# Fourier attention and a mixture of experts: x loaded in quarters, and the early transforms and Nyquist products put in another order

## The reference, cut to what matters

```python
q = layernorm(x) * (scale per token) * (wave per position)
Q, K, V = q @ Wq.T + bq, mem @ Wk.T + bk, mem @ Wv.T + bv
Qf, Kf, Vf = fft(Q), fft(K), fft(V)            # over the 64 positions
QK  = hamilton(Qf * filt, Kf * filt)
QKV = hamilton(QK, Vf * filt)
x = x + ifft(QKV).real
```

## Time and profile before

| | before |
|---|---|
| median of 3 runs | 258.69 us (258.26 to 259.77) |
| the profiled execution | 258.56 us, its trace's span 256.7 us |
| mean granted TensorE clock | 0.895 of full speed |
| busy PE, PEld | 194.5 us (76%), 176.2 us (69%) |
| busy DVE, POOL, ACT | 150.7 us (59%), 142.4 us (55%), 94.5 us (37%) |

### The profile page before, as it was taken

How to read it: one execution, slowest core, us unless ns; L and a number is a source line. 1 busy time by engine, 2 the same in 40 slices (tenths; PEclk the granted TensorE clock), 3 DMA queues, 4 the chain that set the end, 5 groups by cost and what they waited for, 6 DMA issues and landing times.

```text
span 256.7 us, 4792 instructions
## 1 busy us (share of the span) xinstructions
PE 194.5 (76%) x1422; PEld 176.2 (69%) x1422; DVE 150.7 (59%) x405; ACT 94.5 (37%) x235; POOL 142.4 (55%) x237
## 2 busy tenths in 40 slices
PE   8999999999810378788987988698899759969000
PEld 6798877988710357777987977597799659858000
DVE  0888769899888963534443626263475244444255
ACT  0488252214166772413422423242343133233042
POOL 0010689989600057384775867668588757775300
PEclk9999999999965579997997999889999779999755
DMA  7999300000064401011111121102121112122094
GB/s 210 283 412 325 108 0 0 3 1 0 18 198 132 161 20 49 22 43 31 41 41 41 31 51 31 51 22 51 32 43 41 41 41 41 41 43 35 27 349 141
DMA packets 14366, 20.87 MB, mean 81 GB/s; under 512 B 2672, under 2 KB 9360, under 8 KB 14352
## 3 DMA queue, kind: packets, MB, share of 16 engines
q1 hardware_dynamic: 9968, 14.19, 16.9%
q0 software_dynamic: 3008, 5.87, 9.7%
q10 hardware_dynamic: 1376, 0.64, 1.0%
HBM read 15.74 MB, written 4.95 MB: 81 GB/s over the span
## 4 chain that ended last, share of the span: by engine, by line
POOL 24%; DVE 21%; issue 20%; PE 16%; DMA 10%; ACT 3%; DVEq 1%; POOLq 1%; another core or an unknown queue 1%; SPq 0%
POOL y_rows L943 11%; POOL spec L925 10%; DMA y_rows<-spec,lists_now 3%; DVE prod L605 3%; PE bank L1033 3%; DMA xq<-in_x 3%; PE bank L1183 3%; PE bank L1034 3%; POOL taken L920 2%; DMA spec<-xn_rows,lists_now 2%; DVE tok L514 2%; DMA xq<-y_rows 2%; DVE half L626 2%; PE bank L1018 1%; DVE shared_a L755 1%
## 5 line engine op out<-in xcount | busy, mean ns | idle before, releaser
L494 ACT ACTIVATE prod<-bank,b_col 128x256 f32<-128x256 f32 x84 | 37.7, 475 | 90.9 <-PE bank L1173 68.9
L1183 PE MATMUL bank<-w_sb,prod 128*128 128x128 f32 x336 | 50.4, 297 | 17.0 <-DVE prod L808 8.8
L1183 PEld LDWEIGHTS bank<-w_sb,prod 128*128 128x128 f32 x336 | 43.5, 202 | 23.0 <-DVE prod L808 13.3
L808 DVE SCALAR_TENSOR_TENSOR prod<-bank,b_col,prod 128x256 f32<-128x256 f32 x84 | 37.7, 480 | 30.3 <-issue 16.1
L1169 PE MATMUL bank<-xT_hi,w_hi 128*128 128x256 f32 x168 | 51.2, 305 | 0.2 <-issue 0.2
L1173 PE MATMUL bank<-xT_lo,w_hi 128*128 128x256 f32 x168 | 49.1, 292 | 0.0
L1170 PE MATMUL bank<-xT_hi,w_lo 128*128 128x256 f32 x168 | 49.0, 292 | 0.0
L943 POOL DMA_INDIRECT y_rows<-spec,lists_now x42 | 43.4, 1034 | 10.0 <-issue 8.3
L925 POOL DMA_INDIRECT spec<-xn_rows,lists_now x40 | 41.0, 1024 | 9.2 <-issue 8.4
L1169 PEld LDWEIGHTS bank<-xT_hi,w_hi 128*128 128x128 f32 x168 | 34.1, 203 | 0.6 <-issue 0.4
L1173 PEld LDWEIGHTS bank<-xT_lo,w_hi 128*128 128x128 f32 x168 | 33.8, 201 | 0.1
(11 more groups left out here) (181 smaller groups left out, 319.1 us busy)
## 6 DMA issues: line engine op xcount, KB each, us to landing
xq<-in_L_ffn_w SPq DMA_DIRECT2D x2, 1024.0 KB, 4.8
xq<-y_rows SPq DMA_DIRECT2D x2, 640.0 KB, 5.3
xq<-in_x SPq DMA_DIRECT2D x2, 512.0 KB, 6.4
x_sb<-in_L_ffn_w SPq DMA_DIRECT2D x1, 1024.0 KB, 6.8
w_spare<-in_L_ffn_w SPq DMA_DIRECT2D x1, 1024.0 KB, 11.9
xn_rows<-xq SPq DMA_DIRECT2D x4, 256.0 KB, 2.3
xq<-y_rows SPq DMA_DIRECT2D x2, 384.0 KB, 4.9
y_rows<-spec,lists_now POOLq DMA_INDIRECT x42
```

Of the source, the lines that this page charges most:

```text
L494: nc.scalar.activation(silu[:, c, :], bank[:, c, XT:2 * XT], ACT.Silu, bias=b1_col[:, e * 2 * FC + FC + c:e * 2 * FC + FC + c + 1]).then_i ...
L808: stt(act[:, c, :], bank[:, c, 0:XT], b1_col[:, e * 2 * FC + c:e * 2 * FC + c + 1], silu[:, c, :], ALU.add, ALU.mult).then_inc(act_ready, 1)
L1183: last = mm(bank[:, 5 + h, 0:D], act[:, c, h * P:(h + 1) * P], w2_sb[:, e * FC + c, :], start=(c == 0), stop=(c == FC - 1))
```

## The change

Four things are changed, all in the first 35 us. No instruction is computed in another way; two x loads become four.

- SP loads x in four parts of four tiles, each with its semaphore, and DVE takes the statistics part by part. The weights wait for the fourth.
- ACT normalises four tiles, not six, before it copies the spectra of groups 0 and 1; the remaining tiles are parted 4 and 8, not 4 and 6.
- PE puts 4 and 12 of q's Nyquist products after `project(0)` and `project(1)`, where it had 9 and 7. `dft(2)` stands ahead of `project(1)`, and `project(2)` and `dft(3)` stand ahead of the three Nyquist products with the weights.
- ACT's copies follow that order, and `high_part` of experts 2 and 3 comes right after the Nyquist copies.

```diff
-        x_in = [sem(f"x_in{c}") for c in range(2)]
+        x_in = [sem(f"x_in{c}") for c in range(4)]
@@ sync
-            for c in range(2):
-                sp.dma_start(x_sb[:, 8 * c:8 * c + 8, :], x_t[:, 8 * c:8 * c + 8, :]).then_inc(x_in[c], 16)
+            for c in range(4):
+                sp.dma_start(x_sb[:, 4 * c:4 * c + 4, :], x_t[:, 4 * c:4 * c + 4, :]).then_inc(x_in[c], 16)
             sp.dma_start(ctx_sb[:], ctx_t).then_inc(ctx_in_s, 16)
-            sp.wait_ge(x_in[1], 16)
+            sp.wait_ge(x_in[3], 16)
@@ scalar
-            normalise(range(0, 6))
+            normalise(range(0, 4))
             keep_spectra(0, 0)
             keep_spectra(1, 1)
-            normalise(range(6, 10))
+            normalise(range(4, 8))
             keep_q(0, 0)
-            normalise(range(10, NT))
+            normalise(range(8, NT))
             keep_q(1, 1)
+            keep_spectra(2, 0)
             a.wait_ge(nyq_dft, 1)
             nc.scalar.activation(spec_n[:], bank[:, 7, 0:2 * BATCH], ACT.Copy).then_inc(nyq_spec, 1)
-            keep_spectra(2, 0)
+            keep_q(2, 0)
+            keep_spectra(3, 1)
             a.wait_ge(nyq_proj, 1)
...
-            for g in range(2, G - 2):
+            for e in range(2, 4):
+                high_part(e)
+            for g in range(3, G - 2):
                 keep_q(g, g % 2)
                 keep_spectra(g + 1, 1 - g % 2)
-                if g == 2:
-                    for e in range(2, 4):
-                        high_part(e)
@@ vector
-            for c in range(2):
+            for c in range(4):
                 v.wait_ge(x_in[c], 16)
-                for t in range(8 * c, 8 * c + 8):
+                for t in range(4 * c, 4 * c + 4):
@@ tensor
             project(0)
-            nyquist(0, q_sb, range(0, 9))
+            nyquist(0, q_sb, range(0, 4))
+            dft(2)
 
             pe.wait_ge(b1_ready, 1)
             project(1)
-            nyquist(0, q_sb, range(9, NT)).then_inc(nyq_dft, 1)
-            dft(2)
+            nyquist(0, q_sb, range(4, NT)).then_inc(nyq_dft, 1)
+            project(2)
+            dft(3)
             pe.wait_ge(nyq_spec, 1)
...
             for g in range(1, G):
-                if g + 1 < G:
+                if 2 < g + 1 < G:
                     project(g + 1)
-                if g + 2 < G:
+                if 3 < g + 2 < G:
                     dft(g + 2)
```

## The result

| | before | after |
|---|---|---|
| median (lowest to highest) | 259.23 us (258.26 to 259.94, 4 runs) | 270.26 us (266.79 to 271.99, 4 runs) |
| ratio, 95% interval | | 1.038 [1.028, 1.049] |
| repeated (`a1_again`) | 260.22 us (257.58 to 264.59, 23 runs) | 265.65 us (263.95 to 271.9, 6 runs) |
| ratio, 95% interval | | 1.022 [1.016, 1.028] |
| the profiled execution, span | 258.56, 256.7 us | 270.21, 268.4 us |

The change is slower, as forecast, but by 5 to 11 us where 2.1 were forecast. Medians and ranges are of all runs, and the ratios leave out runs more than 1.5% above the fastest of their kernel.

The account below looks back on a forecast made before the run. Bound by a PE and DVE chain, with POOL's nearly as long from `kv_n` to `inverse(5)`. 3.33 - 0.41 - 0.8 = +2.1 us on 258.56 gave 260.7 us; range 259.0 to 262.3.

Parts of the forecast that it names:

- POOL's chain: POOL's work from `kv_n` to `inverse(5)`, a second chain with 0.41 us of slack; its delay was to set the loss, +2.1 us.
- POOL's block: POOL's Nyquist Hamilton products, after waiting for `kv_n`: start 3.33 us later, 35.74 instead of 32.41.
- DVE's wait at the split: At `split_nyquist`, DVE arrives at about 40.0 and waits 2 us for POOL's sums, which come at about 42.0.
- The q basis of group 3 behind the roundings: On ACT, ready at about 36.8 but behind weight roundings ending at about 37.6, so `stage(3)` starts at about 38.0.
- 0.41 + 0.8: Taken off POOL's 3.33 us delay: 0.41 of slack before `inverse(5)`, 0.8 gained by meeting DVE less.
- the head without a fall: Start of the kernel: with four normalised tiles PE goes straight on at 19.37, not 19.84, gaining 0.47 us.
- the scales: DVE's statistics of x in quarters: scales 0.83 us earlier, worth nothing on PE.
- the step-by-step sum of TensorE: PE blocks from `project(0)` on, added in the new order: products with the weights end at 34.69, not 31.36.
- the row of twelve: Twelve of q's small Nyquist products after `project(1)` on PE: 2.54 us, ending at 29.68.
- rival B: PE's clock falls in new waits before `inverse(1)` and `inverse(5)`; the latter costs 1.35 us more: 262.1 us, chance 0.06.
- the late context: The context's load issue moves from 2.02 to about 3.08 behind four x issues; cost to PE taken as 0.
- rival D: At the x loads: quarters land together, changing nothing, or delay the context by the full 0.9 us: 261.6 us; chance 0.08.

Follow-up runs that it names:

- a1_again: The changed kernel run once more, on the chip of its session's other runs: 265.65 us against 260.22 for the kernel before, ratio 1.022.
- e2_order: Changed kernel with x loaded in halves again, new orders of PE and ACT kept: 239.45 us against 236.71 for the kernel before, ratio 1.017.
- t7_early: First layer alone: changed kernel, x in halves, small products parted 9 and 7, weight products and their copies back ahead of `project(2)`: 78.15 us.
- e3_fill: Changed kernel with 30 warm-up matmuls, not 17, ahead of the context's products: 241.09 us against 236.71 for the kernel before.
- t2_after: First layer of the changed kernel alone, cut behind that layer: 83.13 us against 77.92 for the first layer of before.
- t4_order: First layer alone of the changed kernel with x in halves: 82.71 us against 77.92 for the first layer of before.
- t1_before: First layer of the kernel before alone, second layer left out: 77.92 us (77.14 to 82.85, 6 runs).
- t6_row_warm: First layer alone: changed kernel, x in halves, row of twelve kept with six 256-column matmuls put between its products: 82.35 us.
- a3_split: Changed kernel with x in halves and q's small Nyquist products parted 9 and 7 as before: 262.56 us against 260.22 for the kernel before.
- t5_split: First layer alone: changed kernel, x in halves, q's small Nyquist products parted 9 and 7: 80.43 us (79.66 to 85.01, 7 runs).
- e1_quarters: Kernel before with only the x loads in quarters: 239.18 us against 236.71 for the kernel before, ratio 1.000.
- t3_quarters: First layer alone of the kernel before with x in quarters: 77.98 us against 77.92 with x in halves.
- t8_hole: First layer alone: kernel before without the 17 warm-up matmuls ahead of the context's products: 79.75 us (78.32 to 82.21, 6 runs).
- e4_gap: Kernel before with 5 warm-up matmuls, not 17, ahead of the context's products: 237.75 us against 236.71 for the kernel before.

## Why the prediction was right or wrong

**Right: the direction, and POOL's chain.** By `e2_order`, which has the order without a fall in the first layer: from the first projection with `spec` to the end of the products with the weights 15.22 us (19.13 to 34.35; forecast 19.37 to 34.69, 15.32); POOL's block at 35.41 (forecast 35.74); DVE's wait at the split, 2.07 us in the changed kernel (forecast 2); `finish(5)` +2.12 (forecast +2.1). The decisive check is the distance from the start of POOL's block to the end of `finish(5)`, which was the same whatever happened ahead of it: 27.60 us in the profile of the change (42.55 to 70.15), 27.54 in `e2_order`, where before had 28.42. With the products back in their place the delay is gone (`t7_early`). The q basis of group 3 behind the roundings came as said, at 44.20.

That the sum of the chain is met to 0.02 us is luck. In `e2_order` POOL's block moved by 3.00 us and not 3.33, and 0.88 of it was taken up and not 0.41 + 0.8 = 1.21. The two misses cancel. Of the 0.8 that POOL was to gain by meeting DVE less, about half came.

**Right: the head without a fall.** With four tiles, and where the clock stays up, the first projection follows the bias matmul without a wait, at 19.0 to 19.6 (forecast 19.4), but for `e3_fill` with its longer row of warm-up matmuls (21.05). The last quarter of x landed at 8.75, not 8.51, so the scales came 0.47 us earlier (L572 at 16.20) and not 0.83, which TensorE does not feel.

**Wrong: the step-by-step sum of TensorE, with every block at full clock.** A fall of the clock was one rival, with a chance of 0.06. I looked for it only behind the new waits, and priced one inverse, 1.35 us. I left the row of twelve as 2.54 us of busy TensorE and `project(2)` behind it as 2.92, with "no gap" as safe. The row took 2.60 us, but `project(2)` took 4.60. In five of the six profiles that have this row unbroken (the change, `a1_again`, `e3_fill`, `t2_after`, `t4_order`; not `e2_order`) the clock fell in it or within 1.1 us behind it, and in none of the thirteen that have the products parted 9 and 7. That is the 1.7 us of the sum above. `t4_order` has it too: its `finish(5)` ends 4.51 us behind that of `t1_before`, by 2.1 of POOL's chain, 1.7 of this fall, and 0.7 of heads that differ from run to run (its first projection is 0.4 us later than that of `e2_order`, and `t1_before` is 0.3 us ahead of before). That the row's few columns are the cause is not shown (`t6_row_warm`).

**Wrong: the chance of rival B.** TensorE's wait ahead of `inverse(5)` was 2.3 us (forecast 2 to 2.4) in all nine profiles with the Nyquist products behind `project(2)`, and in four of them the clock fell during the wait or up to 1.5 us behind it: `a3_split`, `t4_order`, `t5_split` and `t6_row_warm`. In the profile of the change it did not. From the wait's end to the first matmul with the gate's weights these four took 1.1 to 1.7 us longer than `e2_order`, so my 1.35 was near for one inverse and what follows it. In `t5_split` the clock stayed low for 13 us, through transposes, gate and both last inverses. The residual of group 7 came at 77.23, not 70.44 as in `t1_before`: some 4 us more than POOL's chain explains, three times my price.

**Missed, and not settled: the head.** I took the late context at 0, and it cost 0.6 us in the first profile. There TensorE was also at 1.2 GHz from 15 to 25 us, some 4.5 us of the 11.7, the largest term of the miss. A 1.25 us hole stood ahead of it, made by a context 0.6 us late and weights that TensorE could take up 0.8 us earlier (9.83, not 10.63). I had priced the late context (rival D) at up to 0.9 us, and not a fall of the clock that may follow the hole. Seventeen of the eighteen later profiles have at most 0.43 us of wait there, one has 1.73 us, and none has the fall. What let the clock fall there stays open. A run of `t1_before`, with neither quarters nor a made hole, has a time like one. So the first measurement, +11, had a larger share of these falls than the later ones, +5.4 and +5.2, and what share the quarters have in that is open: alone they cost +2.5 us in the median of `e1_quarters`, nothing in its fastest runs, and nothing in `t3_quarters`.

**The range.** It ended at 262.3 us, and the change took 270.26 and, repeated, 265.65. It was worked out from the terms of a chain on one profiled execution. The falls add a spread of 4 us and more, to the slow side only, and the one trace of before had none in the first layer.

**A misreading without weight.** The prediction says that PE works without a gap but for 0.31 us. Past the shown rows it waits 0.58 us for ACT's `spec`, at 36.04 and again at 40.69. No term of the sum uses this.

## What to carry to other kernels

A chain that the profile's chain of waits does not name can be just as long: add up the engine that never waits (here POOL, with 0.4 us of slack in 28 us), and ask what feeds its first instruction, before delaying that by 3.3 us for a hole elsewhere. On TensorE, price a new order at both clocks, and look at the clock column before believing a busy share. Two places to suspect are a long row of matmuls of a few columns, where parting it is worth a trial, and a wait of 2 us that a new order opens. That matmuls with more columns among the small ones help is likely here and not shown. Where runs fall into clumps, cut the program down to the stage in question: but for one run, `t1_before` spread over 1.1 us, where the whole kernel of before spread over 10.6 in the same session. Run the reference again in every session, in the cut form too, which was not done here for the last two sets.

## What the runs showed of the hardware that was not expected

- The granted clock fell to 1.2 GHz while TensorE was busy without a break: in 24 matmul records of 2 columns (2.6 us) or within 1.1 us behind them in five of six profiles, and at rows of 18 and 14 records in none of thirteen.
- A wait of the same length did not always do the same: 2.3 us of waiting for POOL came with a fall to 1.2 GHz in four of nine profiles, once (`t4_order`) after 2.1 us of the wait itself, once (`t5_split`) followed by 13 us at the low clock. 1.73 us in `t8_hole` left the clock at 2.4 GHz.
- With six matmuls of 0.11 us in the gate's stretch (and ACT's tiles parted 4, 4 and 8) the first layer's five runs lay within 0.53 us of each other (76.52 to 77.05), where six runs of `t1_before`, on another chip, lay 5.7 us apart.
- The expert loop, the same code, took 159 us in the trace of before and 135.5 in `e4_gap`, with `finish(5)` ending at 60.83 and 60.84. On one chip the kernel before took 260.22 us in one session and 235.99 in another.
